# Cross attention and a routed feed-forward on one core: the router's logits computed from the attention's parts inside the attention turns, and the last rows of x loaded earlier

## The reference, cut to what matters

```
x: 16 x 112 x 256, ctx: 16 x 375 x 256, mask over the context
x = x + attention(layernorm(x), ctx, mask)      # 16 heads of 16, Wq Wk Wv Wo with biases
flat = layernorm(x), as 1792 x 256
logits = flat @ router_w                        # 256 x 8 experts
the two best experts of each token, with weights by softmax
out = x + sum over the two of weight * (silu(flat @ w1[e]) @ w2[e])   # 256 to 512 to 256
```

## Time and profile before

| | |
|---|---|
| median of three runs | 455.89 us (455.68 to 457.37) |
| profiled execution | 456.5 us, its span 454.4 us |
| TensorE busy | 416.7 us, 92% of the span |
| VectorE, ScalarE, GpSimd busy | 336.7, 279.7 and 224.3 us: 74%, 62%, 49% |
| granted clock of TensorE, mean | 0.94 of full speed |
| moved by the DMA engines | 64.32 MB, mean 142 GB/s |

### The profile page before, as it was taken

One profiled execution on the slowest core, in us unless ns is written; L12 is line 12 of the kernel. 1 busy time (PEld: TensorE's weight loads), 2 busy tenths in 40 slices (PEclk: granted clock), 3 DMA queues, 4 the chain that ended last, 5 costly groups with the idle time before them and its releaser, 6 DMA issues.

```text
span 454.4 us, 10827 instructions
## 1 busy us (share of the span) xinstructions
PE 416.7 (92%) x4219; PEld 389.6 (86%) x4219; DVE 336.7 (74%) x700; ACT 279.7 (62%) x381; POOL 224.3 (49%) x257
## 2 busy tenths in 40 slices
PE   7859999999999999999999999689999999999920
PEld 7748899999999999999998989679999999999920
DVE  7847578788778887878878778866786677767636
ACT  4637666656666656666645552757877777788600
POOL 6755642124442234431212673765887878785430
PEclk9978999999999999999999995579999999999975
DMA  7955746778666788665560159922222222332169
GB/s 211 227 151 168 171 99 129 146 173 183 168 150 153 144 185 180 135 130 130 111 138 3 55 167 381 305 60 71 80 84 86 90 82 94 79 88 81 46 216 315
DMA packets 44675, 64.32 MB, mean 142 GB/s; under 512 B 6801, under 2 KB 33570, under 8 KB 44626
## 3 DMA queue, kind: packets, MB, share of 16 engines
q1 hardware_dynamic: 38322, 50.40, 44.4%
q0 software_dynamic: 4096, 11.13, 8.2%
q10 hardware_dynamic: 2208, 2.12, 1.4%
HBM read 30.13 MB, written 9.28 MB: 87 GB/s over the span
## 4 chain that ended last, share of the span: by engine, by line
PE 80%; DVE 7%; DMA 5%; ACT 2%; POOL 2%; issue 2%; SPq 1%; ACTq 0%; DVEq 0%
PE ps L1546 41%; PE ps L1609 12%; PE ps L1626 9%; PE ps L1640 9%; PE ps L1915 2%; DVE x L1536 2%; PE ps L1653 1%; DMA y_back<-y_rows 1%; DMA x_rows_sb<-x_rows 1%; PE ps L1719 1%; PE ps L1709 1%; SPq L414 1%; PE ps L1721 1%; DMA keep<-keep_scratch 1%; DMA keep_scratch<-keep_all 1%
## 5 line engine op out<-in xcount | busy, mean ns | idle before, releaser
L1105 DVE TENSOR_REDUCE neg_max<-ps 112x1 f32<-112x376 f32 x256 | 133.8, 546 | 41.2 <-PE ps L1609 36.3
L834 ACT ACTIVATE probs<-ps 125x1344 f32<-125x1344 f32 x64 | 82.8, 1294 | 43.4 <-PE ps L1626 38.2
L1609 PE MATMUL ps<-k_stack,q_stack 98*112 98x376 f32 x256 | 86.6, 374 | 5.9 <-DVE neg_max L1105 5.6
L604 POOL TENSOR_TENSOR k_lo<-k_f,k_hi 128x752 fp32r<-128x752 f32 x16 | 28.9, 1804 | 113.5 <-ACT k_hi L808 112.9
L765 POOL DMA_INDIRECT rows<-xn_rows,token_of_row x42 | 55.8, 1330 | 17.5 <-issue 12.5
L1609 PEld LDWEIGHTS ps<-k_stack,q_stack 98*112 98x112 f32 x256 | 45.3, 179 | 17.2 <-DVE neg_max L1105 12.5
L773 POOL DMA_INDIRECT y_rows<-y_out,slot_of_row x42 | 45.7, 1088 | 25.1 <-ACT y_out L1027 14.2
L1626 PE MATMUL ps<-q_stack,k_stack 100*125 100x224 f32 x384 | 52.7, 273 | 0.0
L1626 PEld LDWEIGHTS ps<-q_stack,k_stack 100*125 100x125 f32 x384 | 50.6, 188 | 0.7 <-ACT probs L834 0.5
L1546 PE MATMUL ps<-w_hi,h_hi 128*128 128x256 f32 x168 | 48.7, 290 | 0.4 <-DVE h_lo L1452 0.4
L1546 PE MATMUL ps<-flat_t_hi,w_hi 128*128 128x256 f32 x168 | 47.6, 283 | 1.3 <-DVE flat_t_lo L1430 1.3
(11 more groups left out here) (213 smaller groups left out, 1031.7 us busy)
## 6 DMA issues: line engine op xcount, KB each, us to landing
k_stack<-k_hi SPq DMA_DIRECT2D x32, 376.0 KB, 4.9
w_all<-w SPq DMA_DIRECT2D x2, 4096.0 KB, 18.5
k_stack<-k_lo SPq DMA_DIRECT2D x16, 376.0 KB, 5.6
ctx_raw<-ctx_t SPq DMA_DIRECT2D x32, 187.5 KB, 3.9
q_stack<-attn_t_hi SPq DMA_DIRECT2D x64, 56.0 KB
y_back<-y_rows SPq DMA_DIRECT2D x14, 256.0 KB, 5.1
x_rows_sb<-x_rows SPq DMA_DIRECT2D x4, 448.0 KB, 4.3
x<-x_tiles SPq DMA_DIRECT2D x7, 256.0 KB, 3.1
```

The costliest lines, as they stand in the source:

```text
L604: pool.tensor_tensor(kl[:, :, :], kf[:, :, :], kh[:, :, :].bitcast(F32), ALU.subtract)\
L834: act.activation(pf[j % 2][:, :, :], ps[0:CT, BK_ST:BK_ST + KT, 0:4 * S], ACT.Exp).then_inc(pf_ready, 1)
L1105: dve.tensor_reduce(neg_max[:, head:head + 1], ps[0:S, BK_MAX + s % 2, 0:CP], AX.X, ALU.max, negate=True).then_inc(max_read, 1)
L1609: pe.matmul(ps[0:S, BK_MAX + a, 0:CP], qs[b.ring][0:R_MAX, a, q, :], ks[b.ring][0:R_MAX, q, :], start=True, stop=True).then_inc(smax_done, 1)
```

## The change

**The load order at the start.** SyncE issues `load_rows(3)` and `load_ctx(first.after(2))` ahead of its wait for `filled`, and loads the output bias once more as columns (`bo_c`).

**The logits.** A row's logits are no longer taken from the normalised row. With c the router with its column means taken off, the logits are rstd times (x @ c + bo @ c + attn @ (Wo transposed times c)), and the mean of the row drops out. Three new steps make the router's forms: `column_means` (TensorE, turn 1), `centre_router` (GpSimd, turn 2), `router_through_output` (TensorE, turn 4: Wo, loaded again by rows, times c), with copies by ScalarE (`copy_sums`) and `router_low` on GpSimd. Then `route(n)` computes a tile: four fp32r products from `th` and `tl` and two plain fp32 products of the transposed input `xt`, to which GpSimd has added the bias (`add_bias_t`). The transposed input is a new array of the host, `x_t`, loaded in seven pieces of 256 KB into three buffers. Eleven tiles are routed in turns 6 to 14 (`ROUTED_IN`), three in the last list; the sums stand in the 64 free columns of `BK_OUT`, four tiles at a time, and ScalarE copies them ahead of `out_copy` (`LOGITS_COPIED`). The logits are not multiplied by rstd until `below_maximum`, as the order of a row's logits does not depend on it.

**The last list.** `flat_transpose`, `flat_high`, `flat_low` and `read_logits` are gone. The early tiles are 12 instead of 8, the order of the last batch's steps on TensorE and VectorE is new, `rank_early` stands before the last group of outputs, GpSimd makes the lanes 10 and 1 instead of 11 and 3, and the rest are VectorE's. `xn2` has three buffers instead of six, and `normalise_rows` and `normalise_late` wait for the store that used the buffer before. The stores of units 6 and 7 are issued by ScalarE instead of SyncE.

```diff
--- before.py
+++ after.py
...
-XN_RINGS = 6
+XN_RINGS = 3
 BK_PROJ = (5, 6, 5, 6, 5, 6, 4, 0)
-BK_FLAT = (3, 5, 3, 5, 1, 2, 3, 5)
-BK_RANK, BK_LATE, BK_PLACED, BK_TOKEN = 4, 6, 7, 0
+BK_RANK, BK_LATE, BK_PLACED, BK_TOKEN = 3, 6, 5, 0
+SUMS = QUADS * S
+SUM_TILES = (512 - SUMS) // (2 * E)
+ROUTED_IN = {6: (0,), 7: (1,), 8: (2,), 9: (3,), 10: (4,), 11: (5,), 12: (6, 7), 13: (8, 9), 14: (10,)}
+LOGITS_COPIED = {9: 0, 12: 1, 14: 2}
 BK_SPIN = 3
-EARLY_NT = 8
-POOL_LANES = (11, 3)
+EARLY_NT = 12
+POOL_LANES = (10, 1)
...
+            sp.dma_start(bo_c[:, :], bo_cols).then_inc(rw_in, 16)
             stack_keys(first)
             stack_queries(first)
             sp.wait_ge(mask_written, 32)
             stack_mask(first)
+            load_rows(3)
+            load_ctx(first.after(2))
             sp.wait_ge(filled, 4)
             stack_queries(second)
             stack_mask(second)
-            load_rows(3)
             stack_keys(second)
-            load_ctx(first.after(2))
...
+            def load_x_t(u):
+                sp.dma_start(xt[u % RINGS][:, :, :], x_t[:, :, TG * u:TG * (u + 1)].rearrange("k p n -> p k n"))\
+                    .then_inc(xt_in[u % RINGS], 16)
+
             for b in range(B):
                 turn(Batch(0, b))
+                if b == 3:
+                    sp.wait_ge(vproj_done, 8)
+                    sp.dma_start(xt[2][:, :, :], wo_rows.rearrange("k p n -> p k n")).then_inc(xt_in[2], 16)
+                    load_x_t(0)
+                    load_x_t(1)
+                if b == 5:
+                    sp.wait_ge(sums_done, 2)
+                    load_x_t(2)
+                if b in (8, 10, 12, 13):
+                    u = {8: 3, 10: 4, 12: 5, 13: 6}[b]
+                    sp.wait_ge(logits_done, 2 * (u - RINGS + 1))
+                    load_x_t(u)
...
-            for u in range(6, 8):
-                write_rows(u)
...
             def normalise_rows(u):
                 pool.wait_ge(row_rstd_ready, u + 1)
-                if u == RINGS:
-                    pool.wait_ge(st_done, QUADS * (B - 1))
+                if u >= XN_RINGS:
+                    pool.wait_ge(xn_written[u % XN_RINGS], 16 * (u // XN_RINGS))
...
+            def centre_router():
+                pool.wait_ge(sums_copied, 1)
+                pool.wait_ge(rw_in, 32)
+                pool.tensor_tensor(rw_raw[:, :, :], rw_raw[:, :, :], router_mean[:, :].rearrange("p (a e) -> p a e", a=1)
+                                   .to_broadcast([P, KD, E]), ALU.subtract).then_inc(router_ready, 1)
+
+            def router_low():
+                pool.wait_ge(sums_copied, 2)
+                pool.tensor_tensor(rw[:, :, E:2 * E], router_f[:, :, :], rw[:, :, 0:E].bitcast(F32), ALU.subtract)\
+                    .then_inc(router_ready, 1)
+
+            def add_bias_t(u):
+                slot = u % RINGS
+                pool.wait_ge(xt_in[slot], 16 * (u // RINGS + 1 + (slot == 2)))
+                for k in range(KD):
+                    last = pool.tensor_scalar(xt[slot][:, k, :], xt[slot][:, k, :], bo_c[:, k:k + 1], None, ALU.add)
+                last.then_inc(xt_ready, 1)
...
+                if b == 0:
+                    pool.memset(mean_of[:, :], 1.0 / D).then_inc(router_ready, 1)
+                if b == 2:
+                    centre_router()
+                if b == 5:
+                    router_low()
+                if b in (5, 6, 7, 10, 12, 13, 14):
+                    add_bias_t({5: 0, 6: 1, 7: 2, 10: 3, 12: 4, 13: 5, 14: 6}[b])
...
+            def copy_sums(b):
+
+                if b == 1:
+                    act.wait_ge(sums_done, 1)
+                    act.copy(router_mean[:, :], ps[:, BK_OUT, SUMS:SUMS + E]).then_inc(sums_copied, 1)
+                if b == 4:
+                    act.wait_ge(sums_done, 2)
+                    through = ps[:, BK_OUT, SUMS:SUMS + KD * E].rearrange("p (k e) -> p k e", k=KD)
+                    act.copy(rw[:, :, 0:E], through)
+                    act.copy(router_f[:, :, :], through).then_inc(sums_copied, 1)
+                if b in LOGITS_COPIED:
+                    part = LOGITS_COPIED[b]
+                    act.wait_ge(logits_done, SUM_TILES * (part + 1))
+                    act.copy(logit_parts[:, SUM_TILES * part:SUM_TILES * (part + 1), :],
+                             ps[:, BK_OUT, SUMS:512].rearrange("p (n e) -> p n e", n=SUM_TILES)).then_inc(logits_read, 1)
+
             def out_copy(b):
                 act.wait_ge(pv_done, QUADS * (b.n + 1))
+                copy_sums(b.n)
...
+            def write_late_rows(u):
+                act.wait_ge(late_xn_ready, u - 5)
+                store_rows(act, u)
...
+            write_late_rows(6)
             for k, c in enumerate((1, 0)):
                 places_in_block(k, c, slice(0, EARLY_NT))
             places_in_block(TOP, 1, slice(EARLY_NT, NT))
+            write_late_rows(7)
...
             def normalise_late(u):
                 dve.wait_ge(row_rstd_ready, u + 1)
-                dve.wait_ge(xn_written[u % XN_RINGS], 16)
-                dve.wait_ge(ft_done, u - XN_RINGS + 1)
+                dve.wait_ge(xn_written[u % XN_RINGS], 16 * (u // XN_RINGS))
...
+            def sum_early():
+                dve.wait_ge(logits_read, len(LOGITS_COPIED))
+                sum_logits(slice(0, EARLY_NT), logit_parts)
+
+            def sum_late():
+                dve.wait_ge(logits_done, NT)
+                late = NT - EARLY_NT
+                sum_logits(slice(EARLY_NT, NT), ps[:, BK_OUT, SUMS:SUMS + 2 * E * late].rearrange("p (n e) -> p n e", n=late))
...
             def below_maximum():
                 step(dve.tensor_reduce(c0[:, :], logits[:, :, :], AX.X, ALU.max))
-                dve.tensor_tensor(shifted[:, :, :], logits[:, :, :], wide2(c0), ALU.subtract).then_inc(shifted_ready, 1)
+                step(dve.tensor_tensor(t0[:, :, :], logits[:, :, :], wide2(c0), ALU.subtract))
+                dve.wait_ge(row_rstd_ready, len(UNITS))
+                dve.tensor_tensor(shifted[:, :, :], t0[:, :, :], wide2(row_rstd), ALU.mult).then_inc(shifted_ready, 1)
...
             last = Batch(0, B - 1)
             row_vars(2)
-            flat_low(0)
             residual(4)
             row_vars(3)
-            read_logits(0)
+            row_vars(4)
             normalise(last.after(-1))
+            sum_early()
+            find_two(early_tiles)
             attn_low(last.after(-1))
-            row_vars(4)
             residual(5)
-            flat_low(1)
             row_vars(5)
             residual(6)
-            read_logits(1)
             row_vars(6)
-            flat_low(2)
+            normalise(last)
+            place_rows(0, early_tiles, BK_RANK)
+            attn_low(last)
             normalise_late(6)
-            normalise(last)
-            flat_low(3)
-            read_logits(2)
-            flat_low(4)
-            attn_low(last)
-            read_logits(3)
-            find_two(early_tiles, 4)
             residual(7)
+            count_early()
+            sum_late()
+            find_two(late_tiles)
             row_vars(7)
-            flat_low(5)
-            flat_low(6)
-            normalise_late(7)
-            place_rows(0, early_tiles, BK_RANK)
-            flat_low(7)
-            read_logits(4)
-            read_logits(5)
-            count_early()
-            read_logits(6)
-            read_logits(7)
-            find_two(late_tiles, 8)
             lanes(0)
             place_rows(1, late_tiles, BK_LATE)
             lanes(1)
             late_places_in_block()
             count_blocks()
             blocks_of_lanes()
+            normalise_late(7)
             below_maximum()
             read_lanes()
             list_tokens()
...
+            def column_means():
+
+                pe.wait_ge(router_ready, 1)
+                pe.wait_ge(rw_in, 32)
+                product(ps[:, BK_OUT, SUMS:SUMS + E], [(mean_of[:, :], rw_raw[:, k, :]) for k in range(KD)])\
+                    .then_inc(sums_done, 1)
+            def router_through_output():
+
+                pe.wait_ge(router_ready, 2)
+                pe.wait_ge(xt_in[2], 16)
+                for j in range(KD):
+                    last = product(ps[:, BK_OUT, SUMS + E * j:SUMS + E * (j + 1)],
+                                   [(xt[2][:, k, P * j:P * (j + 1)], rw_raw[:, k, :]) for k in range(KD)])
+                last.then_inc(sums_done, 1)
...
+            def route(n):
+
+                if n == 0:
+                    pe.wait_ge(router_ready, 3)
+                newest = (P * (n + 1) - 1) // S
+                pe.wait_ge(th_ready, KD * (newest + 1))
+                pe.wait_ge(tl_ready, KD * (newest + 1))
+                pe.wait_ge(xt_ready, n // 2 + 1)
+                m, half = slice(P * n, P * (n + 1)), slice(P * (n % 2), P * (n % 2 + 1))
+                at = SUMS + 2 * E * (n % SUM_TILES)
                 for k in range(KD):
-                    for a in range(n):
-                        at = P * (n * k + a)
```

(55 more changed lines are left out.)

94 lines of the change are left out of this document (26 added, 68 removed).

## The result

The changed kernel takes 465.97 us (median of four, 464.62 to 467.47), the kernel before 456.56 (455.68 to 457.37): a ratio of 1.0207, 95% interval 1.0167 to 1.0247. The forecast was 459.0 in a range of 454.0 to 462.5. The direction was right, the size was not.

A forecast was written before the change was run, and what follows sets the result against it. It took a start gap, a full TensorE in the attention turns and a tail of hand-overs as bounds. 456.5 - 4.1 + 12.4 - 5.2 = 459.6 for the profiled execution, 459.0 for the median, range 454.0 to 462.5.

The forecast's parts named there:

- The last rows: At the start, load_rows(3) and load_ctx(2) ahead of SP's wait for filled: -4.1 us, between -3 and -4.7.
- The price of a product: In the turns, two weight loads of 0.111 us per plain fp32 product; eight loads, 0.89 us, for a routed tile.
- the four passes: True fp32 takes four passes; if each loaded its weights, a tile would cost 1.33 us and the turns 6.2 more.
- The broken pair: Insertions split the two output groups at a turn's border: 1.4 to 2.6 us in 11 turns, taken as 1.7.
- No slack in the turns: The attention turns are TensorE's own list, so whatever is added there is paid in full; turns +12.4 us.
- Rival 2: The turns absorb the new products in 0.7 us of slack each: 451.3, or 455.2 at half; chance 0.12.
- The loads in the turns, costed at nothing: Eight loads of 256 KB, covered at DMA share 0.71; up to 2 us for a late stack in the range.
- The tail: Behind the last attention batch, lanes filled 5.2 us sooner, and table, weights and first expert with them; bounds -7.6 and -2.7.
- Rival 3: In the tail, the first gather waits for unit 7 and store 4 before it; 3 us late, 462.0; chance 0.16.
- Rival 4: The clock falls inside the turns, some 1.7 us for each of nine, 474; chance 0.04; unnumbered in the prediction.
- The rule on queues: Each DMA engine serves queue rows with work in turn, so ScalarE's store would not stand behind SP's 4 MB.

## Why the prediction was wrong

- **The last rows** (-4.1): right in its sum, in part by luck. Turn 0 ends 3.84 sooner in the changed kernel and 4.1 sooner with this part alone. I had 3.81 at the statistics, at about 28.2, and 0.3 from the clock. The statistics came at 28.95 with this part alone, 3.0 sooner, because VectorE's maxima ahead of them ended 0.9 later than before; the other 1.1, for which I had allowed up to 0.8, goes with the clock. Two errors of 0.8 cancel.
- **The price of a product**: right. A plain fp32 product with 8 columns is two loads; all products of a tile come to 0.82, I had 0.89. The chain of the changed kernel shows a tile: four fp32r products, then two fp32 products as four records in 0.45.

```profile
145.63 0.21 PE ps L1754
145.84 0.11 PE ps L1755
145.95 0.12 PE ps L1754
146.06 0.11 PE ps L1755
146.17 0.45 PE ps L1757 x4
```

  By the estimate that I worked out from the four passes of the Trainium skill (FP8 and Floating Point Precision, "TensorE Precision Notes"), with a weight load for each pass, those two would have taken 0.89; the measurement decides, and it is half of that.
- **The broken pair** (1.7 for eleven turns): too small. It is 0.31 a turn, 3.4.
- **No slack in the turns**: right. Rival 2 falls: the second routing of a tile added 0.92 to a turn (15.78 less 14.86).
- **The loads in the turns, costed at nothing**: this step failed. I took 0.71 of DMA share as the cover and put up to 2 us into the range for a late stack. With the loads the share was 0.80 from their issue to the mask's (98.9 to 108.9) and 0.98 from there to its landing. A mean share says what the DMA engines have left over some turns; what counts is what stands behind a load in its queue. SyncE's queue carries the stacks, whose last piece had 5.7 us ahead of its use, and three loads in one place used them up. And a wait of 2.3 us costs 5.0, since the clock falls behind it: I had bounded the wait, not the half clock that follows.
- **The tail** (-5.2): right to the table: -4.43, and the eleventh tile in front of it is 1.13, so -5.6. ScalarE's places were the last arrival at the fills, as I had laid out: they take 10.15 us (289.18 to 299.33; I had 10.4), the fills 5.5 at half clock (0.50 from 299 to 305 us; I had 5.9). ScalarE's timeline in the changed kernel, first and last step of the places:

```profile
289.18 3.61 ACT L1025 ACTIVATE is_place<-numbers,in_block 128x128 fp32r<-128x128 f32 x12 [1.93 <-DVE xn L1335]
...
297.85 1.48 ACT L1029 ACTIVATE is_place<-is_place 128x1536 fp32r<-128x1536 f32 x1
```

  TensorE's fills in the same kernel:

```profile
299.38 5.49 PE L1922 MATMUL ps<-is_place,placed 128*112 128x128 f32 x28 [4.48 <-ACT is_place L1029]
```

- **Rival 3**, a new wait that eats the tail, came on top: the first gather did wait for unit 7, which VectorE normalises only behind the lanes. It was held by that place in VectorE's list, not by store 4 on SyncE's queue: `normalise_late(7)` followed its predecessor without a wait, and ScalarE's store landed 5.32 us after its issue beside the second expert load. My layout had the place right: unit 7 normalised 2.4 us ahead of the end of the fills (288.5 and 290.9), and its store was issued 2.4 ahead (302.45 and 304.87). What had no price in the sum was the landing: the list is ready 1.25 us behind the fills, so the store had 3.7 us and took 5.32. I gave it 0.16 as a case of its own; it was a term of the sum.
- **Rival 4**, the clock that falls inside the turns, with TensorE busy: I gave it 0.04, as nine falls of some 1.7. The profiled execution of the result has none behind a routing block, so that it is not part of the sum below; but single falls of 1.5 to 1.6 came in four of the six traces with blocks of two tiles, and five in the kernel that routes every tile twice.
- **The rule on queues** that I weighed for rival 3 (the Trainium skill, DMA: Bandwidth & Descriptors, "Queues, rings and completion order") says that a DMA engine serves the queue rows with work in turn. The two kernels with three loads agree: on ScalarE's row they do not hold SyncE's stacks (457.00 against 459.47, part of which is SyncE's issuing and can be the earlier start). I used the rule for the store alone; the same rule speaks against putting prefetches into the row of the stacks.

In sum the forecast for the profiled execution, 459.6, missed 5.0 for the mask, 1.9 for the gather, 0.7 in the turns (13.1 without the mask's 5.0, against 12.4), 0.8 in the experts and 0.3 at the start, against 0.4 gained in the tail and 0.3 outside the span: 8.0, and 467.47 is 7.9 above it. The 0.8 in the experts is unexplained and need not be the change: the same steps take between 149.1 and 151.1 in the traces here.

## What to carry to other kernels

Before a prefetch is put into a queue, look at which transfer stands behind it and how far ahead of its use that one is issued; the mean DMA share does not show it, and a queue that carries nothing urgent took the same bytes for nothing here. In a list that an engine works off without gaps, price an insertion with what it breaks, the pair or the pipeline at its place, and try it at the neighbouring places. A wait of TensorE costs more than its length where the clock falls behind it: 5.0 for 2.3 us and 2.9 for 1.5 us here.

## What the runs showed of the hardware

- The granted clock fell from 1.00 to 0.50 without any wait of TensorE, for about 3 us, right behind blocks of 16 or 32 weight loads in a row: in five of nine turns where every tile was routed twice, in four of six traces with two such blocks. What decides on it in one execution and not in the next, no run here shows.
- Three loads of 256 KB cost 2.5 to 3 us in the queue of the stacks (459.47 against 456.29) and nothing measurable in another queue at about the same time (457.00 against 456.36), with the DMA engines as busy.
